# Two- and four-bank slots for the exps of an attention, a held-back weight load and an inverse root by Newton steps

## The reference

```python
# c: what a small mixture of experts (gate by the condition, 4 experts, top 2, one shared) makes of x
qkv = (c @ w_qkv.T).reshape(B, N, 3, 16, 16)            # 16 heads of width 16
q, k = rms_norm(q), rms_norm(k)                         # t * rsqrt(mean(t*t) + 1.19e-7), per head
attn = softmax(einsum('bhnd,bhmd->bhnm', q, k) * 16 ** -0.5)
y = einsum('bhnm,bhmd->bhnd', attn, v)
y = y - sum(y * Vn) * Vn                                # Vn: v over its own norm
x2 = x + y.reshape(B, N, C) @ w_proj.T
x3 = (decaying state over the sequence, gated by tanh) @ Wo + bo      # two taps, softplus, scan
route = sigmoid(x3 @ Wr + br)                           # 8 experts, each token takes the largest
out = x2 + max(route) * (gelu(x3 @ W1[e]) @ W2[e])      # e: the token's expert
```

## Time and profile before

| | us |
|---|---|
| median of 3 runs | 846.78 (845.64 to 847.67) |
| the profiled execution: device time | 847.82 |
| the profiled execution: span of the trace | 846.1 |
| TensorE busy | 782.2 (92%) |
| ScalarE busy | 526.1 (62%) |
| VectorE busy | 460.7 (54%) |
| GpSimd busy | 248.0 (29%) |
| exps of the attention: first start to last end | 328.51 to 584.71 |

### The profile page before, as it was taken

One profiled execution on the slowest core, in us unless ns is written; L12 is line 12 of the kernel. 1 busy time (PEld: TensorE's weight loads), 2 busy tenths in 40 slices (PEclk: granted clock), 3 DMA queues, 4 the chain that ended last, 5 costly groups with the idle time before them and its releaser, 6 DMA issues.

```text
span 846.1 us, 13449 instructions
## 1 busy us (share of the span) xinstructions
PE 782.2 (92%) x4456; PEld 511.0 (60%) x4456; DVE 460.7 (54%) x828; ACT 526.1 (62%) x699; POOL 248.0 (29%) x308
## 2 busy tenths in 40 slices
PE   8999999998999999888999999998799699999995
PEld 5778888887777875233222222223645488888884
DVE  4887666388766641533201202112447479999994
ACT  4432222463232237978999999997445188888883
POOL 5434444134434305100000001000000347777762
PEclk9999999999999999799999999999999799999998
DMA  9131111001243045064551353100189621111000
GB/s 249 18 77 51 50 50 50 26 25 49 77 149 100 1 67 84 0 117 167 67 76 32 44 74 53 21 0 0 50 304 379 238 83 49 52 51 52 26 11 0
DMA packets 52674, 64.87 MB, mean 77 GB/s; under 512 B 15889, under 2 KB 43929, under 8 KB 52636
## 3 DMA queue, kind: packets, MB, share of 16 engines
q1 hardware_dynamic: 44564, 55.96, 26.1%
q0 software_dynamic: 3312, 6.31, 2.4%
q10 hardware_dynamic: 4760, 2.12, 0.9%
HBM read 51.52 MB, written 15.60 MB: 79 GB/s over the span
## 4 chain that ended last, share of the span: by engine, by line
PE 66%; ACT 12%; DVE 9%; issue 8%; DMA 3%; ACTq 0%; SPq 0%; POOLq 0%; DVEq 0%
PE psum L1573 44%; ACT pexp L872 9%; PE psum L1725 8%; PE psum L1713 4%; PE psum L1929 2%; DMA x_d<-x_tm 2%; PE psum L1843 1%; DVE hl L1021 1%; DVE hh L1170 1%; PE psum L1779 1%; DMA x_tm<-in_x 1%; DVE yT L1269 1%; PE psum L1676 1%; PE psum L1829 1%; DVE ssum L1210 1%
## 5 line engine op out<-in xcount | busy, mean ns | idle before, releaser
L872 ACT ACTIVATE pexp<-psum 128x1024 f32<-128x1024 f32 x256 | 237.8, 1086 | 15.4 <-PE psum L1713 15.4
L799 ACT ACTIVATE hid<-psum,b_col 128x512 f32<-128x512 f32 x96 | 66.0, 689 | 160.8 <-PE psum L1573 107.6
L1725 PE MATMUL psum<-pexp,v_ones 128*32 128x512 f32 x1024 | 138.8, 615 | 18.4 <-ACT pexp L872 11.6
L1713 PEld LDWEIGHTS psum<-q_stack,k_stack 48*128 48x128 f32 x512 | 39.7, 188 | 111.9 <-ACT pexp L872 94.3
L1170 DVE TENSOR_SCALAR hh<-hid,scale_col 128x341 fp32r<-128x341 f32 x192 | 69.3, 402 | 69.7 <-ACT hid L799 52.8
L1713 PE MATMUL psum<-q_stack,k_stack 48*128 48x512 f32 x512 | 96.8, 453 | 7.2 <-DVE parts L1263 3.5
L1021 DVE SCALAR_TENSOR_TENSOR hl<-hid,scale_col,hh 128x341 fp32r<-128x341 f32 x192 | 96.3, 543 | 3.4
L1573 PE MATMUL psum<-hh,w2h 128*128 128x512 f32 x192 | 76.4, 398 | 3.4 <-DVE hl L1021 3.2
L1573 PE MATMUL psum<-x_hi,w1h 128*128 128x512 f32 x192 | 77.0, 401 | 0.7 <-DVE x_lo L1035 0.6
L1573 PE MATMUL psum<-hh,w2l 128*128 128x512 f32 x192 | 75.0, 391 | 0.0
L1573 PE MATMUL psum<-x_hi,w1l 128*128 128x512 f32 x192 | 74.9, 390 | 0.0
(11 more groups left out here) (277 smaller groups left out, 1477.9 us busy)
## 6 DMA issues: line engine op xcount, KB each, us to landing
w_all<-in_L_ffn_W SPq DMA_DIRECT2D x16, 1024.0 KB, 13.7
raw<-in_L_cond_ew SPq DMA_DIRECT2D x32, 256.0 KB, 3.3
parts_d<-parts SPq DMA_DIRECT2D x8, 1024.0 KB, 5.0
q_stack<-parts_d SPq DMA_DIRECT2D x48, 128.0 KB, 4.7
k_stack<-parts_d SPq DMA_DIRECT2D x48, 128.0 KB, 7.6
raw<-in_L_cond_sw SPq DMA_DIRECT2D x16, 256.0 KB, 3.3
x_d<-x_tm SPq DMA_DIRECT2D x2, 1024.0 KB, 5.0
x_d<-x_tm ACTq DMA_DIRECT2D x4, 512.0 KB, 11.8
```

Source lines behind the costliest of these rows:

```text
L799: act.activation(hid[k % 4][:], bank(k % 4), ACT.Gelu_apprx_tanh, bias=b1_col[:, bass.ds(4 * q + k // 2, 1)]).then_inc(gelu_done, 1)
L872: act.activation(pexp[mt % 2][:, 2 * j:2 * j + 2, 512 * h:512 * h + 512], psum[:, 2 * r:2 * r + 2, :], ACT.Exp, scale=D ** -0.5)\
L1713: ins = pe.matmul(psum[:, 2 * r + lane, :], k_stack[i][rows, j, mt * P:(mt + 1) * P], q_stack[i][rows, j, 512 * h:512 * h + 512], start=Tr ...
L1725: ins = pe.matmul(psum[VW * j:VW * j + VW, 6 + h, :], v_ones[i][:, mt, j, :], pexp[mt % 2][:, j, 512 * h:512 * h + 512], start=(mt == 0), ...
```

## The change

**Slots for the exps.** Banks 4 and 5 are now one slot of two banks, banks 0 to 3 one slot of four. `cycles(g)` cuts the 32 units of a group into cycles of three: one unit to the two-bank slot, two units to the four-bank slot, each slot emptied by one exp (`exp_units`, 1024 and 2048 columns). A hole takes the upper half (banks 2 and 3) of the four-bank slot, which then holds one unit. Groups 2 to 7 have 11 cycles with one hole, group 0 has 11 cycles with one hole, group 1 has 12 with four. `values_at(g)` lays the calls of `values()` between the scores, two at most in a cycle. `pexp` is one ring of nine units (`place`), and `qk_tm`, `yT` change places in memory for it.

**Newton steps.** `inverse_root()` on VectorE takes the place of the second root: a start value by shift and subtraction on the integers, then four Newton steps, 18 instructions of 128 x 256 in all. `root()` stays for the first sequence.

**Held back.** SyncE waits for `x3_stored` before it loads expert 4. And VectorE makes the low part of the first tile's x (`x_lo_part(0, 0)`) ahead of the weights of tile 1.

```diff
-        def turns(g):
...
+        def holes(g):
+            if isinstance(g, int) and g == 0:
+                return {10: ("qk", 0)}
+            if isinstance(g, int) and g == 1:
+                return {3: ("qk", 1), 5: ("qk", 2), 7: ("turn", 0), 10: ("qk", 3)}
+            return {5: ("turn", 0)}
+
+        def cycles(g):
+            hole, out, u = holes(g), [], 0
+            while u < UNITS:
+                four = [u + 1] if len(out) in hole else [u + 1, u + 2]
+                out.append((u, four, hole.get(len(out))))
+                u += 1 + len(four)
+            assert u == UNITS
+            return out
...
+        def values_at(g):
+            out, v, c = {}, 0, cycles(g)
+            for k in range(1, len(c)):
+                for n, last in ((0, c[k - 1][0]), (1, c[k - 1][1][-1])):
+                    if v < UNITS // 2 - 2 and 2 * v + 1 <= last:
+                        out[k, n] = v
+                        v += 1
...
             for e in range(spare, RE - under_route):
+                if e == 4:
+                    sp.wait_ge(x3_stored, 16 * 2 * NB)
                 load_expert(e)
...
             def exps(g):
...
-                    if isinstance(g, int) and g == 0 and u == 19:
-                        root(1)
+                for c, (two, four, _) in enumerate(cycles(g)):
+                    exp_units(g, [two], 4)
+                    exp_units(g, four, 0)
...
+            def inverse_root():
+                ms, r, t = ssum[:, :, 0:2 * H], inv_root[0], inv_root[1]
+                dve.wait_ge(var_made, 2)
+                nlink(dve.tensor_scalar(r[:].bitcast(I32), ms.bitcast(I32), 1, None, ALU.arith_shift_right))
+                nlink(dve.tensor_scalar(r[:].bitcast(I32), r[:].bitcast(I32), -1.0, float(0x5f3759df),
+                                        ALU.mult, ALU.add))
+                for _ in range(4):
+                    nlink(dve.tensor_tensor(t[:], r[:], r[:], ALU.mult))
+                    nlink(dve.tensor_tensor(t[:], t[:], ms, ALU.mult))
+                    nlink(dve.tensor_scalar(t[:], t[:], -0.5, 1.5, ALU.mult, ALU.add))
+                    nlink(dve.tensor_tensor(r[:], r[:], t[:], ALU.mult))
...
             dve.wait_ge(x3_stored, 16 * 2 * NB)
+            x_lo_part(0, 0)
             w1_lo_parts(1, place_of_expert(dve, 1))
-            x_lo_part(0, 0)
             x_lo_part(1, 1)
...
+                for c, (two, four, next_hole) in enumerate(cycles(g)):
+                    after(pe, exp_done, base + 2 * c - 1)
+                    scores(i, two, 4)
+                    give_values(c, 0)
+                    after(pe, exp_done, base + 2 * c)
+                    if hole and hole[0] == "qk":
+                        pe.wait_ge(part_lo, 8 + hole[1] + 1)
+                    elif hole:
+                        pe.wait_ge(y_read, g)
+                    for n, u in enumerate(four):
+                        scores(i, u, 2 * n)
+                    if next_hole and next_hole[0] == "qk":
+                        turn_b(next_hole[1])
+                    elif next_hole:
+                        turn(g - 1)
+                    hole = next_hole
+                    give_values(c, 1)
...
-            values(GROUPS - 1, 1, LT - 1, 0)
-            values(GROUPS - 1, 1, LT - 1, 1)
+            for n in range(2):
+                pe.wait_ge(exp_done, exps_before(GROUPS) - 1 + n)
+                values(1, UNITS // 2 - 2 + n)
```

More of the change, by code:

```diff
@@ L153, in layer_kernel @@
         at = [stage]
-        qk_tm = [sb(f"qk_tm{b}", [P, LT, 2 * C], F32, at) for b in range(NB)]
-        x_at, x_hi, x_lo = [], [], []
+        qk_tm, x_at, x_hi, x_lo = [None, None], [], [], []
         for b in range(NB):
+            qk_tm[1 - b] = sb(f"qk_tm{1 - b}", [P, LT, 2 * C], F32, at)
             x_at.append(at[0])
@@ L1735, in group @@
                     pe.wait_ge(stack_in[i], 16 * LOADS * (g - i) + 16 * 2 * LOADS)
-                order = turns(g)
-                for pos, (what, u) in enumerate(order):
-                    pair_free(g, order, pos)
-                    if what == "turn":
-                        turn(g - 1, pos % 3)
-                    elif what == "qk":
-                        turn_b(u, pos % 3)
-                    else:
-                        scores(i, u, pos % 3)
-                        mt, j = u // HG, u % HG
-                        if j % 2 and first and mt == 0:
-                            pe.matmul(psum[:, 6 + j // 2, :], ident[:], projT[:].rearrange("p k c -> p (k c)"),
-                                      start=True, stop=True)
-                        elif j % 2:
-                            if mt == 0:
-                                values(g - 1, 1 - i, LT - 1, j // 2)
-                            else:
-                                values(g, i, mt - 1, j // 2)
+                base, at, hole = exps_before(g), values_at(g), holes(0).get(10) if isinstance(g, int) and g == 1 else None
@@ L1797, in _ @@
                 if w == 0:
-                    turn(GROUPS - 1, 1)
+                    turn(GROUPS - 1)
             for w in range(4):
```

119 lines of the change are left out of this document (58 added, 61 removed).

## The result

The changed kernel takes 855.59 us (median of 6 runs, 854.34 to 856.51), the kernel before, run beside it, 847.16. The ratio of the paired runs is 1.0094, 95% interval 1.0078 to 1.0110: slower by 8.0 us (6.6 to 9.3); the two medians by themselves are 8.4 apart. The forecast was 848.0 us and its range ended at 854.5.

The account below looks back on a forecast made before the run. ScalarE's exps were taken to bound the attention, only a little, with TensorE close behind. The terms +12.0 - 1.9 - 0.9 - 7.3 = +1.9 (floor +0.4) put 1.2 onto the 846.8 median: 848.0 us, 8-in-10 range 842.5 to 854.5.

Parts of the forecast that it names:

- The slots in the loop: Six attention loop groups: distances between four-bank scores of 2.71 or 3.09 us, 32.5 against 30.5 a group, +12.0 us.
- Groups 0 and 1: First two attention groups, outside the loop: 71.3 us against 73.2, -1.9 us, with the second root's gain included.
- The root and the Newton steps: Second root on ScalarE: loads, root and low-clock waits go, 5.9 us; the 8.3 us of VectorE steps stay hidden.
- The end of the attention: Last values calls: the first of them waits only for the exp before the last, -0.9 us.
- The held weights: First tile after the attention: x3 stored before the tokens, gather and turn_h(0) earlier, -7.3 us, between -8.8 and -3.
- I take 1.5 in all for the first two: First two gathers, running beside the released weights: 1.4 us more for each gather of 128 KB, 1.5 counted in all.
- so the clock should stay high: TensorE at the first tile: rows arrive as filling work ends, no 0.50 clock; 1.7 us off the 9.4 to turn_h(0).
- The lower bound of -3: Smallest gain at the first tile, -3 us: four gathers one behind the other, each 1.4 us longer beside weights.
- Rival 1: Attention: two-slot hand-off costs more, distances of 2.78 to 2.80 instead of 2.71; 852, at worst 856 us; chance 0.27.
- Rival 2: Attention and tail: hand-off hidden at 2.68, gathers undelayed, values calls partly overlapping; -3.6, 843.2 us; chance 0.25.
- rival 4: Tail: x3 stored no earlier because ScalarE's queue is slow, so the -7.3 goes; 855 us; chance 0.03.
- Rival 3: Attention: TensorE's clock falls because it waits in every cycle; one group so is 19 us; 865 us; chance 0.03.

Follow-up runs that it names:

- before + Newton, 4 to 7 late: Kernel before with Newton steps, experts 4 to 7 loaded after the first three gathers, first tile's low part of x moved ahead: 838.30 us, ratio 0.9898.
- split release: Kernel before with Newton steps, low part of x first, expert 4 released when x3 is stored, 5 to 7 after the first three gathers: 834.71 us.
- before + weights held: Kernel before with only experts 4 to 6 held until x3 is stored and the first tile's low part of x moved ahead: 843.98 us, ratio 0.9965.

## Why the prediction was wrong, point by point

- **The slots in the loop: right.** Predicted 3.09 and 2.71 for the two distances, 3.88 over the hole and 32.5 us for a group; measured 3.08, 2.73 on average (2.69 to 2.79), 3.87 and 32.58. An exp of 2048 columns was bounded at 1.87 by rows and took 1.88; the Trainium skill (ScalarE: Activation LUTs, What ACT_TABLE_LOAD costs) gives 1.89, and the trace agrees. That TensorE's work sets the longer distance is shown by the run with half the columns, 30.68 us a group.
- **Groups 0 and 1: right, the exact sum in part luck.** 71.3 predicted, 266.8 - 6 x 32.58 = 71.3 measured. The four holes for q and k took 4.18 or 4.19 each and not 4.09.
- **The root and the Newton steps: right in the mechanism, the size in part luck.** -5.9 predicted for the root; 6.4 us less in the exps than in the profile that the prediction was read from, but only 3.8 less than in another execution of the same attention, whose low clock was shorter; -4.9 (2.6 to 7.1) in the time. The steps are hidden on VectorE. The switch costs 3.04 us with two loads; the drain of 1.38 us for each load, which the same section of the Trainium skill states, would have made the gain 2.8 larger and is not in the rows.
- **The end of the attention: right.** The first context copy moved by 597.03 - 587.37 = 9.7 us while the last exp's end moved by 10.5, which with rounding is -0.9.
- **The held weights: the step that failed.** Predicted -7.3, measured -3.2 in the span. That x3 would be stored before the tokens was right (3.6 us before). Two terms of the sum were too small. "I take 1.5 in all for the first two" gathers, at 1.4 each by the store of x3: the first one took 3.5 us longer than before's, and its rows were turned 7.7 us after the tokens instead of 3.9 + 1.5 = 5.4 (the gather is issued 1.15 us after `token_s` begins where I had 0.24, which the old wait for x3 had hidden; and it takes 6.5 us, over the 6 that the prediction gave as its mark of being wrong). And "so the clock should stay high": a gather that is late leaves TensorE dry, and the clock then makes 7.6 us into 9.5. Together 2.3 + 1.8 = 4.1. The lower bound of -3, four gathers at 1.4, had the right size by luck: it was one gather, turned 7.7 - 3.9 = 3.8 us late, and 1.8 of clock (-8.8 + 3.8 + 1.8 = -3.2). Both were named; they were set one by one at their kind ends, although the low clock came with the late gather. The Trainium skill (DMA: Bandwidth & Descriptors, Queues, rings and completion order) pointed to the -3 end, by a DMA engine that drains a whole packet of one queue before it turns to the next. The gather's 6.3 to 6.7 us beside 375 to 384 GB/s agree with that; that packets are the reason, no run here shows.
- **The range.** It ended 1.1 us short of the median. With -3.2 in place of -7.3 and +12.5 in place of +12.0 for six groups, the sum is +6.5, and on the median before, 846.8 + 6.5 = 853.3, inside. Of the other 2.3 us, 0.5 lie between attention and tail and 0.4 in the kernel before, whose median was 847.2 this time; the rest is the scatter of executions, for which the range had no room at its upper end.
- **The rivals.** Rival 1 (hand-off) didn't happen at its price: two of the six distances with one call are at 2.78 or 2.79, the others at 2.69 to 2.71. Rival 2 and rival 4 didn't happen either (x3 was stored 3.6 us ahead of the tokens). Rival 3 did not happen in after, but it did in the kernel with half the columns.

## What to carry to other kernels

Two buffers with wide operations save a part of the engine's fixed cost (a pair of exps for three units every 2.70 us, where three exps took 3 x 0.915 = 2.745) but put every hand-off on the path, and TensorE's unevenness with it: the ring of three absorbed the values call of 1.00 us that stands between two pairs of score units, two slots did not absorb the 1.00 + 1.00 us of two such calls. When a transfer is moved out of the way of another, list every transfer that is awaited in its new place: 6 MB held back for a store delayed the gather behind it, and all of it later delayed the next one; a third place, one load of 2 MB early and three after the first gathers, gave 13 us with the Newton steps. And where a late transfer also leaves TensorE dry, price both: after the wait of 3.79 us for the first gather its clock was 0.50 for the next 5 us. A cost that is read from one profile of before can itself be one of several: the second root cost 6.4 us in one execution and 3.8 in another.

## What the runs showed of the hardware

- The four matmuls of a values call, each in its own strip of 32 columns of TensorE, run together: four take 1.06 us (after), two 1.05 (after with half the matmuls). The Trainium skill (TensorEngine Tiling (Array Packing), Key Properties) says that tiles operate independently; the rows agree. Leaving out two of the four saved nothing.
- An indirect gather of 128 rows that TensorE waited for took 3.0 to 3.5 us from its issue to its use when little else moved and 6.3 to 6.7 us beside weights at 375 to 384 GB/s.
- After waits of 1.12 and 0.99 us TensorE's granted clock was 0.50 in the stretch from 658 to 660 (split release, five keep-warm matmuls); after 0.68 and 0.99 it stayed at 1.00 (before + Newton, 4 to 7 late).
- After the same stop of TensorE at the second root (2.57 and 2.56 us) the granted clock was near 0.50 for 10 us in before and for 4 us in before + weights held.
- With less to do, TensorE was slower in one execution: with half the columns in 12 of 16 values calls, its clock was 0.50 from 420 to 440 us, and the span 5.9 us longer than with all of them.
